# The 7x7 depthwise convolution of a two-layer metaformer: DVE taps replaced by banded matmuls, layer-norm stages moved by one chunk

## The reference, cut to what matters

```python
x = x + attention(ln_c(x))                 # depthwise 3x3 convs, deformable sampling, linear attention
t = t + ffn(ln_t(t))                       # 4 experts 96->384->96, gelu, gates of the best two
x = x + (dw(x1,w77) + dw(x1,w53) + dw(x1,w35)      # x1 = ln_c(x), layer norm over channels
         + dw(dw(x1,w7w),w7h) + dw(dw(x1,w5w),w5h) + b77 + b53 + b35)
t = t + ffn(ln_t(t))
```

## Time and profile before

| | us |
|---|---|
| median of 3 runs (1854.15 to 1859.1) | 1855.65 |
| the profiled execution, as timed | 1861.07 |
| its span in the trace | 1859.3 |
| PE busy / DVE busy in the span | 1400.2 / 1346.9 |
| ACT busy / POOL busy | 724.0 / 303.3 |
| mean granted clock of TensorE (share of 2.4 GHz) | 0.911 |

### The profile page before, as it was taken

One profiled execution on the slowest core, in us unless ns is written; L12 is line 12 of the kernel. 1 busy time (PEld: TensorE's weight loads), 2 busy tenths in 40 slices (PEclk: granted clock), 3 DMA queues, 4 the chain that ended last, 5 costly groups with the idle time before them and its releaser, 6 DMA issues.

```text
span 1859.3 us, 21000 instructions
## 1 busy us (share of the span) xinstructions
PE 1400.2 (75%) x5452; PEld 890.5 (48%) x5452; DVE 1346.9 (72%) x3073; ACT 724.0 (39%) x1436; POOL 303.3 (16%) x304
## 2 busy tenths in 40 slices
PE   2121623469879787787997899869987998899898
PEld 1010222335545454545554565546654665566565
DVE  1689398448874698547999799979998899443332
ACT  2130223225543354433444344434444344455443
POOL 1014013301150013201121112202121001000000
PEclk9999955589899899898998899989998999899999
DMA  2522213132421425123121421142213111221111
GB/s 66 130 53 59 74 45 90 37 109 68 118 75 30 139 67 145 56 83 93 58 62 42 149 68 56 45 146 61 66 49 113 45 52 42 79 70 60 53 59 48
DMA packets 105037, 137.66 MB, mean 74 GB/s; under 512 B 46070, under 2 KB 97144, under 8 KB 104184
## 3 DMA queue, kind: packets, MB, share of 16 engines
q1 hardware_dynamic: 98344, 131.20, 24.0%
q0 software_dynamic: 3072, 4.82, 1.1%
q10 hardware_dynamic: 3536, 0.63, 0.2%
HBM read 96.99 MB, written 39.62 MB: 73 GB/s over the span
## 4 chain that ended last, share of the span: by engine, by line
PE 32%; DVE 29%; issue 8%; POOL 6%; ACT 3%; DMA 1%; DVEq 1%; ACTq 0%; POOLq 0%
PE y_ps L815 15%; DVE acc L1106 9%; DVE part L1020 4%; PE h_ps L833 3%; PE h_ps L835 3%; PE h_ps L834 3%; POOL ln_rstd L730 3%; PE at_ps L920 3%; DVE ln_stats L994 3%; ACT ln_tok L598 2%; PE at_ps L851 2%; DVE pair L1026 2%; POOL ln_bias L733 2%; DVE ln_mv L1001 2%; PE lb_ps L794 1%
## 5 line engine op out<-in xcount | busy, mean ns | idle before, releaser
L629 ACT ACTIVATE hidden<-h_ps,b 128x448 f32<-128x448 f32 x672 | 421.5, 636 | 625.5 <-PE h_ps L835 619.5
L815 PE MATMUL y_ps<-hidden,w 128*96 128x448 f32 x1344 | 647.0, 567 | 19.1 <-ACT hidden L629 18.7
L1106 DVE SCALAR_TENSOR_TENSOR acc<-xq,all_w,acc 128x756 f32<-128x756 f32 (+2 forms) x504 | 475.9, 998 | 10.4 <-DMA xq<-norm_c 10.4
L833 PE MATMUL h_ps<-xh,w1h 96*128 96x448 f32 (+1 forms) x672 | 474.7, 706 | 0.0
L730 POOL TENSOR_TENSOR ln_rstd<-ln_ve,minus_half 112x4 f32<-112x4 f32 x112 | 154.7, 1382 | 1370.8 <-DVE ln_ve L1005 1362.7
L1020 DVE SCALAR_TENSOR_TENSOR part<-y_ps,b,gate_t 96x448 f32<-96x448 f32 x224 | 151.7, 677 | 298.9 <-PE y_ps L815 265.1
L794 PE MATMUL lb_ps<-ident,ln_tok 112*96 112x112 f32 x448 | 80.0, 312 | 332.5 <-ACT ln_tok L598 332.5
L598 ACT ACTIVATE ln_tok<-lt_ps,ln_bias,ln_rstd 112x96 f32<-112x96 f32 x448 | 156.3, 429 | 356.1 <-POOL ln_bias L733 332.1
L815 PEld LDWEIGHTS y_ps<-hidden,w 128*96 128x96 f32 x1344 | 211.2, 170 | 138.7 <-ACT hidden L629 52.7
L834 PE MATMUL h_ps<-xl,w1h 96*128 96x448 f32 (+1 forms) x672 | 251.0, 374 | 0.0
L835 PE MATMUL h_ps<-xh,w1l 96*128 96x448 f32 (+1 forms) x672 | 250.0, 372 | 0.0
(11 more groups left out here) (114 smaller groups left out, 1133.0 us busy)
## 6 DMA issues: line engine op xcount, KB each, us to landing
gate_t<-gates_dram SPq DMA_DIRECT2D x112, 336.0 KB, 3.3
xq<-norm_c SPq DMA_DIRECT2D x16, 420.0 KB, 4.9
xq<-norm_a SPq DMA_DIRECT2D x16, 336.0 KB, 4.1
ln_x_c<-in_x SPq DMA_DIRECT2D x28, 168.0 KB, 2.4
norm_a<-ln_cm_c SPq DMA_DIRECT2D x28, 168.0 KB, 2.0
x_res<-in_x SPq DMA_DIRECT2D x4, 1176.0 KB, 9.5
value_pairs<-pixels SPq DMA_DIRECT2D x4, 1176.0 KB
x_attn<-x_res SPq DMA_DIRECT2D x4, 1176.0 KB, 6.2
```

Source lines behind the costliest of these rows:

```text
L629: act.activation(hidden[c % HID_RING][:, :], h_ps[c % H_BANKS][:, 0:TILE], ACT.Gelu, bias=b1[l][:, c:c + 1]).then_inc(gelu_done, 1)
L815: pe.matmul(y_ps[e % Y_BANKS][0:C, 0:TILE], w2[l][:, c, :], hidden[c % HID_RING][:, :], start=(j == 0), stop=(j == CPE - 1)).then_inc(hid_ ...
L833: pe.matmul(ps, hi, xh[:, cols], start=True, stop=False)
L1106: step(g, dve.scalar_tensor_tensor(dst, src, w, dst, ALU.mult, ALU.add))
```

## The change

The convolution is laid out anew: 6 groups of channels times 20 input rows stand on 120 partitions (`xt`), and a matmul with a 120x84 banded matrix makes 6 channels times 14 output rows for one kernel column `dx`; the moving side is 4 bands of rows times up to 56 columns (224 at most). An image takes 16 groups times 7 `dx` = 112 such matmuls. Two groups share a fill of `at_ps`, eight fills an image; DVE adds fill, bias and `acc` in two instructions (`add_fill`). The taps, `middle_column`, `diag` and `add_bias` go. PE's fill `f` takes chunks 11+9f to 17+9f of the slot's 84, two matmuls at each.

The banded matrices are made once, in conv slot 0: PE spreads the taps with a selection matrix (`make_toeplitz`, 14 matmuls in 4 rounds), DVE masks them into place (`spread_taps`, 12 instructions in those rounds, 9,408 elements per partition in all). The taps go through DRAM in the slot of ffn 0 (`load_taps`, 20 small DMAs on SP). To save room, `xt`, `acc` and the matrices share memory with the attention's buffers.

The input of an image is now loaded by ACT's queue (`load_band`): four hooks, at chunks 0 to 3 of the first tile, each with six DMAs of 20x16 runs of 224 bytes. SP's store of `acc` and its load are six DMAs each of 14x64 runs of 224 bytes. Both loads of `acc` for images 0 and 1 now stand in conv slot 0.

Norms, in every slot: lnc goes in at chunk 1 instead of 2 and is scaled at 5, back at 6, moved at 7; lnf goes in at 7 instead of 8; in a slot's last tile lnc goes in at 1 instead of 3 and lnf is scaled at 10 instead of 9. On DVE `normalize0` now stands ahead of `combine0`.

```diff
-        STAGES = {"c": dict(turn_in=2, apply=6, turn_back=7, move=8), "f": dict(turn_in=8, apply=11)}
+        STAGES = {"c": dict(turn_in=1, apply=5, turn_back=6, move=7), "f": dict(turn_in=7, apply=11)}
-            ORDER = ("combine0", "split", "normalize0", "combine1", "combine2", "normalize1", "combine3", "sum",
+            ORDER = ("normalize0", "combine0", "split", "combine1", "normalize1", "combine2", "combine3", "sum",
...
+            def load_acc(b):
+                for i in range(CG):
+                    sp.dma_start(acc_rows(b, i), band_rows(x_ffn0[b], i)).then_inc(acc_ld[b], 16)
+            def store_conv(b):
+                sp.wait_ge(at_free, AT_CONV + FILLS * (b + 1))
+                for i in range(CG):
+                    sp.dma_start(band_rows(x_conv[b], i), acc_rows(b, i)).then_inc(conv_st[b], 16)
...
+            def load_band(b, r):
+                if r == 0:
+                    act.wait_ge(norm_st["c", b], 16 * TILES)
+                    if b == 0:
+                        act.wait_ge(a_step, A_ALL * NB)
+                    else:
+                        act.wait_ge(at_free, AT_CONV + FILLS * b)
+                for i in range(CG):
+                    src = norm["c"][b].rearrange("(c g) (y x) -> c y g x", c=CG, x=SIDE)[i, r * QROWS:r * QROWS + BAND]
+                    act.dma_start(xt[i * BAND:(i + 1) * BAND, :, r, :], src).then_inc(xt_ld, 16)
...
+                start = {} if slot["ffn"] is None else {1: [exp_scores], GATES_TURN: [take_gates]}
+                if slot["conv"] is not None:
+                    for r in range(BANDS):
+                        start[r] = start.get(r, []) + [lambda r=r: load_band(slot["conv"], r)]
...
+                def conv_fill(f, i):
+                    b = slot["conv"]
+                    if i == 0:
+                        pe.wait_ge(at_free, AT_CONV + FILLS * b + f)
+                        if f == 0:
+                            pe.wait_ge(xt_ld, 16 * CG * BANDS * (b + 1))
+                    for n in (2 * i, 2 * i + 1):
+                        g, dx = 2 * f + n // 7, (3, 0, 1, 2, 4, 5, 6)[n % 7]
+                        x0, x1 = max(0, 3 - dx), SIDE - max(0, dx - 3)
+                        ps = at_ps[0:K_OUT, g % 2 * XCOLS:(g % 2 + 1) * XCOLS].rearrange("p (r x) -> p r x", x=SIDE)
+                        last = pe.matmul(ps[:, :, x0:x1], toep(g, dx), xt[:, g, :, x0 + dx - 3:x1 + dx - 3],
+                                         start=(n % 7 == 0), stop=(n % 7 == 6))
+                    if i == 6:
+                        last.then_inc(at_full, 1)
...
-            def conv_taps(slot, m):
...
+            def add_fill(b, f):
+                dve.wait_ge(at_full, AT_CONV + FILLS * b + f + 1)
+                if f == 0:
+                    dve.wait_ge(acc_ld[b], 16 * CG)
+                for g in (2 * f, 2 * f + 1):
+                    ins = dve.scalar_tensor_tensor(acc[b % 2][:, g, :], at_ps[0:K_OUT, g % 2 * XCOLS:(g % 2 + 1) * XCOLS],
+                                                   bias_c[:, g:g + 1], acc[b % 2][:, g, :], ALU.add, ALU.add)
+                ins.then_inc(at_free, 1)
```

More of the change, by code:

```diff
@@ L503, in _ @@
                 if slot["before"] is not None and slot["before"]["conv"] is not None:
-                    b = slot["before"]["conv"]
-                    sp.wait_ge(c_step, C_ALL * (b + 1))
-                    for q in range(Q):
-                        sp.dma_start(x_conv[b].rearrange("(g c) (q n) -> q c g n", g=G, q=Q)[q],
-                                     acc[b % 2][q::Q]).then_inc(conv_st[b], 16)
+                    store_conv(slot["before"]["conv"])
                 if slot["ffn"] is not None:
@@ L705, in _ @@
                     4: {3: [tanh], **{KEY_TURNS + i: [take] for i, take in enumerate(takes[AT_KEY:])}},
-                    6: {1: [take_kv], **{2 + g: [lambda g=g: take_m2(g)] for g in range(G)}}}, behind)
+                    6: {1: [take_kv], **{2 + g: [lambda g=g: take_m2(g)] for g in range(G)}}})
                 if slot is SLOTS[0]:
@@ L709, in _ @@
                     act.copy(all_w[:, :], at_ps[:, 0:CONV_W]).then_inc(taps_set, 1)
-                if slot["conv"] is not None and slot["conv"] + 1 < NB:
-                    add_bias(slot["conv"] + 1)
         N_CONST, N_TAPS = const_count[0], taps_count[0]
@@ L925, in _, with make_toeplitz @@
-                if slot["conv"] is not None:
-                    table = {m: {5 + dy: [lambda m=m, dy=dy: middle_column(m, dy)] for dy in range(7)}
-                             for m in range(PIECES)}
-                    for c, hooks in beside_first.items():
-                        table[0][c] = hooks + table[0].get(c, [])
+                def make_toeplitz(i):
+                    pe.wait_ge(at_free, AT_GEN + i)
+                    if i == 0:
+                        pe.wait_ge(pick_ld, 16 * CG)
+                        pe.wait_ge(toep_ld, 16 * 2 * CG)
+                    rows = range(i * GEN_RO, min(QROWS, (i + 1) * GEN_RO))
+                    for j, ro in enumerate(rows):
+                        last = pe.matmul(at_ps[0:K_IN, j * CGROUPS * 7:(j + 1) * CGROUPS * 7],
+                                         pick[:, QROWS - 1 - ro:QROWS - 1 - ro + K_IN], taps_cd[:, :],
+                                         start=True, stop=True)
+                    last.then_inc(at_full, 1)
@@ new lines, in _ @@
+                if slot["conv"] is not None:
+                    table = {m: {} for m in range(TILES)}
+                    if slot["conv"] == 0:
+                        for i in range(GEN):
+                            c = LATE_Y + max(0, i - 1)
+                            beside_first[c] = beside_first.get(c, []) + [lambda i=i: make_toeplitz(i)]
+                    table[0] = beside_first
+                    for f in range(FILLS):
+                        for i in range(7):
+                            m, c = divmod(FILL_FIRST + FILL_PITCH * f + i, CHUNKS)
+                            table[m].setdefault(c, []).append(lambda f=f, i=i: conv_fill(f, i))
@@ L1129, in _ @@
                                      combine3=10, sum=4, sum_experts=4, sum_residual=4, split_last=4)
+            before_fill = [f"combine{e}" for e in range(E)]
+            FILL_COMBINE = 5
             def body(m, part_of, beside):
@@ L1135, in body @@
                     ops = attn_taps(slot, m, part_of)
-                if slot["conv"] is not None:
-                    ops = conv_taps(slot, m)
                 jobs = ln_jobs(slot, m)
@@ L1158, in body @@
                     if name in work:
+                        if slot["conv"] is not None and name in before_fill:
+                            f, left = divmod(E * m + before_fill.index(name) - FILL_COMBINE, 3)
+                            if left == 0 and 0 <= f < FILLS:
+                                add_fill(slot["conv"], f)
                         done += share[name]
@@ L1330, in _ @@
                     dve.wait_ge(xq_ld, 16 * Q * (b + 1))
-                if slot["conv"] is not None:
-                    dve.wait_ge(xq_ld, 16 * Q * (NB + slot["conv"] + 1))
-                    dve.wait_ge(c_bias, G * (slot["conv"] + 1))
+                if slot["conv"] == 0:
+                    dve.wait_ge(toep_ld, 16 * 2 * CG)
+                    for i in range(GEN):
+                        spread_taps(i)
                 if slot["ffn"] is not None and slot["ffn"] > 0:
```

206 lines of the change are left out of this document (105 added, 101 removed).

## The result

The changed kernel takes 1888.47 us (median of 4 runs, 1881.38 to 1890.65), the kernel before 1855.32 on the same chip: a ratio of 1.0169, 95% interval 1.0138 to 1.0199. It is slower, by 1.7%, and above the range that was given (1799 to 1884). The profiled execution took 1887.54 us with a span of 1885.7, 26.4 more than in the earlier trace rows.

What follows compares the result with a forecast made beforehand. DVE was taken to set the conv slots' pace, PE close behind. Savings of 7 (conv slots), 7, 5 and 2, less 2 for `load_taps`, made 19 us: profiled 1861.07 to 1842, median 1855.65 to 1837; range 1799 to 1884.

Steps and rivals of the forecast that it cites:

- Tiles 1 to 6 of a conv slot: PE's work with banded matmuls plus 2.3 us of waits takes 154.5 us, no better than 153.0 before.
- The relief of DVE by itself is thus worth nothing: In tiles 1 to 6, 119 us of taps leave DVE, but the relief is bought with PE time.
- the sum of conv slot 3: Six tiles at 150.0 and a first tile at 35.4 make 185.4 us against 182.95, a loss of 2.4.
- The first tile: Conv slots 1 and 2: earlier statistics outweigh a gates' store 5.3 us later; tile sum after 36.4 us, against 41.4.
- Gelu 6 and the turn-back are done when the gates come: First conv tile: early `normalize0` removes the 6.2 us that pass between combine and next gelu.
- The sums' loads: Conv slot 0: 12 DMAs for `acc` at 1.3 us, 16 us on SP; 4 us of wait counted.
- The matrices in slot 0: PE's 14 small matmuls cost 2.7 us; DVE's 10.6 us of spreading is covered by its wait for the gates.
- Band issues: ACT issues 18 band DMAs before the gates' store, 0.69 us each, 4.1 for six.
- the cheap bound: Rival: band DMAs at 0.34 us each, 3.6 us saved in each of four slots, 1823 us; chance 0.16.
- the slower rival: Bands share engines with SP's store of `acc`, 1.3 us a DMA on ACT: 44 us in all, 1881; chance 0.22.
- load_taps: Start of ffn 0: some 20 issues of 0.34 us on SP and a wait, 2 us counted against.
- The norm stages elsewhere: Savings outside conv slots: 7 us in ffn 0 and 1, 5 in the two-norm slot, 2 in ffn 6.

Runs made afterwards that it cites:

- e3_acc_late: Changed kernel with the loads of the next image's sums issued on SP behind the first tile's work, not ahead of tile 1's loads: 1868.90 us, 1.0055.
- e5_taps_late: Changed kernel with the 20 small tap transfers of the first feed-forward slot issued behind its first tile's work: 1876.01 us, 1.0079.
- e8_spread: Changed kernel with sums' and taps' loads behind the first tile, store in halves, bands in 48 half transfers, some a slot early: 1822.57 us, 0.9787.
- e6_bands_later: Changed kernel with each image's 24 band loads issued at chunks 4 to 7 of the first tile instead of 0 to 3: 1952.44 us, 1.0476.
- e12_later_both: Changed kernel with bands at chunks 4 to 7 and the next image's sums loaded behind the first tile: 1887.65 us, 1.0152.
- e4_no_bands: Changed kernel without the 24 band loads of images 1 to 3, their convolution computed from image 0's rows: 1862.98 us, 1.0018.

## Why the prediction was wrong

It had -19 us in the profiled execution and the change brought +26.4. The step that failed is the wait: the prediction priced the new transfers by the time of their issues, and let PE run from `combine0` to the tile's sum, and through tile 1, with no wait for a load but 4 us in slot 0. Measured, PE waits there for the norms' loads, which stand behind and beside the sums' loads. By its own steps:

- **Tiles 1 to 6 of a conv slot: right.** 154.5 predicted, 153.9 measured. A chunk with a banded pair takes 2.09 us from start to start (below), 0.72 more than without one, predicted 0.732:

```profile
1099.59 0.71 PE L880 MATMUL h_ps<-xh,w1h 96*128 96x448 f32 x1
...
1101.68 0.71 PE L880 MATMUL h_ps<-xh,w1h 96*128 96x448 f32 x1
```

  "The relief of DVE by itself is thus worth nothing" held in these tiles. So did the sum of conv slot 3, 185.4 against 185.95, with 1.6 us too little for its first tile and 1.1 too much for the others.
- **The first tile: a wait that was left out.** 36.4 us was predicted for slots 1 and 2 and 35.4 for slot 3; 43.6, 39.3 and 37.0 came. The gates' store was to be 5.3 us later and was 8.5 later in slot 1 (20.35 us behind the last pair sum, before 11.9), `combine0` stood at 27.1 us behind it against 26.1. So the gates themselves cost 1 us more than forecast. "Gelu 6 and the turn-back are done when the gates come" nearly held: they start at 1054.10 and 1053.87, `combine0` at 1054.08. The real miss is what follows: 16.5 us pass from `combine0` to the pair sum, against 10.3. PE stops 2.35 us for `ln_x_f` and then works 6 us at half clock, which is 3 us more than at full clock (estimate), where 1 was counted. `e3_acc_late`, which takes the sums' loads away from `ln_x_f`, brings the 16.5 down to 12.3. Not all of that is the load, though: `e5_taps_late` leaves the sums' loads where they are, PE stops 1.4 us for `ln_x_f` and stays at full clock behind it, and the stretch takes 13.8 us. What it gains there it loses in tile 1, so that the first two tiles of slot 1 take 70.7 us together, 69.7 in the changed kernel and 64.5 in `e3_acc_late`. The norms' own loads were never put on the path. In slots 2 and 3, where PE stops 0.9 and 0 us for `ln_x_f`, it is 12.7 and 11.4 us.
- **The sums' loads: mis-sized and misplaced.** 1.3 us an issue was estimated, 2.1 is the median. The delay of tile 1 was counted in slot 0 alone, at 4 us; it was 7.4 there (33.5 against 26.05) and 8.6 in slot 2. Slots 0 and 2 miss by 14 and 11 us (214.9 against 200.7, 201.8 against 190.9). `e3_acc_late` shows this term at 20.7 us in the three slots. It is the largest single miss.
- **The matrices in slot 0: a cover that didn't hold.** The prediction let DVE spread the taps "while it would wait for the gates anyway". Its 200.7 is 9.8 above the 190.9 of slot 1, and it names only 2.7 and 4 of that. PE's rounds and DVE's alternate, each waiting for the other, from 832 to 849 us, and the statistics and `combine0` stand behind them:

```profile
832.93 0.86 DVE L1160 TENSOR_TENSOR toep_own<-at_ps,group_of 120x672 f32<-120x672 f32 x1 [2.00 <-PE at_ps L965]
...
848.27 0.76 DVE L1160 TENSOR_TENSOR kon_mem<-at_ps,group_of 120x588 f32<-120x588 f32 x1
...
850.37 0.67 DVE L1090 SCALAR_TENSOR_TENSOR part<-y_ps,b,gate_t 96x448 f32<-96x448 f32 x1
```

  `combine0` comes 38.3 us behind the pair sum there, 7.1 after its `gate_t` has landed; in slot 1 that is 0.1. In `e8_spread` the two numbers are 34.3 and 9.1, so this part doesn't come from the bursts. No run here takes it away.
- **Band issues.** 0.69 us each was taken, and 0.42 is the median, near the cheap bound; it is 1.11 for the third six. The sum for the first 18 was right by luck: 12.3 us forecast, 12.2 measured in slot 1, 5.5 for twelve and 6.7 for six. The mechanism of the slower rival, bands and SP's transfers on shared engines, was the right one. That the time ended within 8 us of its 1881 is luck too: its 44 us were put on ACT's issues alone, while most of the loss sat in the loads that PE waits for. The Trainium skill, DMA: Bandwidth & Descriptors, section Issuing engines are not separate DMA queues, says that transfers started by different engines run on the same DMA engines and interleave; `e6_bands_later` against `e12_later_both` agrees with it: 65 us between the two medians, 3.2 points.
- **`load_taps`: 2 us counted, 7.7 measured** (812.08 against 804.39). It named 20 issues and a wait. The wait was mis-sized: the round trip of two small stores alone is 11.3 us on SP's queue.
- **The norm stages elsewhere: right in direction, too large in size.** 12 us were counted up to the end of ffn 1 (7 and 5). The first pair sum of ffn 0 comes 8.15 us sooner, and without the taps' load in the way (`e5_taps_late`) ffn 1 ends 8.2 us sooner, no more. The taps' load took that back. In ffn 6 the later tiles give 0.55 us each, 3.5 in all, but the first one loses 5.5 to the store of the last image, which no step had priced.

Sum of the measured parts: -0.5 up to ffn 1, +25.0 in the conv slots, +2.0 in ffn 6, -0.15 in ffn 7: 26.4.

What stays open: why runs of the same 224 bytes go at different rates. Windows of `e4_no_bands` while the sums' loads (14 partitions of 64 runs) were in flight, and of the changed kernel while band loads (20 partitions of 16 runs) and one store of a tile were:

```profile
1053.00:1057.00 4.00, 4.00 (x12) 2.44 (x11) 1.38 (x10) 0.63 (x1) 1.21 (x2) 0.58 1.23 89
```

```profile
1227.00:1229.00 2.00, 0.00 (x0) 0.00 (x0) 1.23 (x4) 1.02 (x2) 0.00 (x0) 0.95 0.84 175
```

89 GB/s against 175, over 4 and 2 us. Longer windows are nearer to each other: 96 GB/s over 12 us (1050 to 1062 of `e4_no_bands`) and 140 over 8 us (1225 to 1233 of the changed kernel), both with other transfers in them. The number of engines that serve each, the pattern of addresses and the direction were not told apart.
